# A reordered opening for a gated cross-attention and mixture-of-experts block: first loads on two queues, key spreading on GpSimd

## The reference

```python
def reference(x, ctx, g_xattn, g_ffn, ...):
    # cross-attention: 16 heads of 16 features, 77 context tokens per batch
    q = split_heads(layernorm(x) @ W_q.T + b_q)
    k = split_heads(ctx @ W_k.T + b_k)
    v = split_heads(ctx @ W_v.T + b_v)
    probs = softmax(einsum('bhsd,bhtd->bhst', q, k) / sqrt(16))
    x = x + tanh(g_xattn) * (combine(einsum('bhst,bhtd->bhsd', probs, v)) @ W_o.T + b_o)
    # feed-forward: a shared expert and two of seven routed ones per token
    h = layernorm(layernorm(x)) * ln_g + ln_b
    top_vals, top_idx = top_k(h @ Wr, 2)              # gates = softmax(top_vals)
    # each expert takes at most 732 (token, choice) slots
    routed = scatter_add(gate * (silu(xe @ W1) * (xe @ W3)) @ W2)
    shared = silu(h @ W1s) * (h @ W3s) @ W2s
    return x + tanh(g_ffn) * (routed + shared)
```

## Time and profile before

| what | us |
|---|---|
| median of 3 runs (878.12 to 883.29) | 878.38 |
| the profiled execution | 886.02 |
| its span, first to last instruction | 883.8 |
| PE busy | 839.1 (95%) |
| DVE busy | 590.3 (67%) |
| ACT busy | 387.7 (44%) |
| POOL busy | 320.2 (36%) |

### The profile page before, as it was taken

The page is one execution under the profiler, slowest core; times in us unless marked ns, Lnnn a source line. Parts: engine busy times, 40 slices in busy tenths (PEclk is TensorE's granted clock), DMA queues, the critical chain, the costliest instruction groups (busy, mean ns, idle before and its releaser), DMA issues.

```text
span 883.8 us, 14663 instructions
## 1 busy us (share of the span) xinstructions
PE 839.1 (95%) x5262; PEld 729.9 (83%) x5262; DVE 590.3 (67%) x1292; ACT 387.7 (44%) x717; POOL 320.2 (36%) x243
## 2 busy tenths in 40 slices
PE   8788999999999999999999999999999999999991
PEld 7465685886858868688688899999999999999990
DVE  4565768878778787888877576565656657565340
ACT  5425426345363263533725445353544445453330
POOL 4830303033012150031224603818375472814333
PEclk9788799999999999999999999999999999999996
DMA  6632041311412214112130722334434332431111
GB/s 227 163 72 64 11 120 36 98 35 39 119 37 66 65 38 119 36 39 62 33 120 11 215 84 80 65 106 95 114 83 86 101 79 69 101 65 20 17 19 19
DMA packets 93984, 66.93 MB, mean 76 GB/s; under 512 B 55110, under 2 KB 80892, under 8 KB 93928
## 3 DMA queue, kind: packets, MB, share of 16 engines
q1 hardware_dynamic: 40312, 55.40, 22.1%
q0 software_dynamic: 53088, 10.30, 8.5%
q10 hardware_dynamic: 528, 0.52, 0.2%
HBM read 37.38 MB, written 14.27 MB: 58 GB/s over the span
## 4 chain that ended last, share of the span: by engine, by line
PE 81%; issue 3%; ACT 3%; DVE 3%; POOL 1%; DMA 0%; DVEq 0%; ACTq 0%; POOLq 0%
PE bank L1608 21%; PE bank L1610 21%; PE bank L1609 21%; PE bank L1840 3%; PE bank L1841 2%; PE bank L1842 2%; PE bank L1732 2%; PE bank L1726 2%; DVE row_max L1278 2%; PE bank L1696 2%; ACT float_data L1100 1%; ACT probabilities L1100 1%; PE bank L1882 1%; PE bank L1794 1%; PE bank L1803 1%
## 5 line engine op out<-in xcount | busy, mean ns | idle before, releaser
L1608 PE MATMUL bank<-split_operands 128*128 128x366 f32 (+4 forms) x1148 | 383.6, 334 | 4.0 <-POOL split_operands L919 2.3
L1609 PE MATMUL bank<-split_operands 128*128 128x366 f32 (+4 forms) x1148 | 377.8, 329 | 0.0
L1610 PE MATMUL bank<-split_operands 128*128 128x366 f32 (+4 forms) x1148 | 377.6, 329 | 0.0
L1608 PEld LDWEIGHTS bank<-split_operands 128*128 128x128 f32 (+1 forms) x1148 | 215.6, 188 | 24.3 <-issue 9.0
L1610 PEld LDWEIGHTS bank<-split_operands 128*128 128x128 f32 (+1 forms) x1148 | 215.4, 188 | 12.3
L1609 PEld LDWEIGHTS bank<-split_operands 128*128 128x128 f32 (+1 forms) x1148 | 215.8, 188 | 9.6
L1018 POOL DMA_INDIRECT out<-float_data,scatter_now x42 | 125.7, 2994 | 185.6 <-DVE float_data L1571 108.7
L1591 DVE TENSOR_TENSOR hidden<-bank,float_data 128x366 f32<-128x366 f32 x112 | 60.4, 540 | 114.1 <-PE bank L1610 114.1
L1197 ACT ACTIVATE float_data<-bank 128x366 f32<-128x366 f32 x112 | 53.5, 477 | 113.7 <-PE bank L1610 113.7
L1194 ACT CAST split_operands<-hidden 128x366 fp32r<-128x366 f32 x112 | 55.7, 497 | 68.4 <-DVE hidden L1591 68.4
L993 POOL DMA_INDIRECT float_data<-z_scratch,gather_now x42 | 72.8, 1733 | 17.4 <-issue 16.2
(11 more groups left out here) (156 smaller groups left out, 1062.9 us busy)
## 6 DMA issues: line engine op xcount, KB each, us to landing
float_data<-in_L_ffn_W SPq DMA_DIRECT2D x21, 1024.0 KB, 8.7
split_operands<-split_operands SPq DMA_DIRECT2D x96, 128.0 KB, 2.3
float_data<-in_x SPq DMA_DIRECT2D x8, 512.0 KB, 4.3
z_scratch<-float_data SPq DMA_DIRECT2D x8, 512.0 KB, 3.1
out<-float_data SPq DMA_DIRECT2D x7, 512.0 KB, 2.9
split_operands<-split_operands SPq DMA_DIRECT2D x8, 192.0 KB, 3.8
float_data<-in_L_ffn_W1s SPq DMA_DIRECT2D x2, 512.0 KB, 9.8
float_data<-in_L_ffn_W3s SPq DMA_DIRECT2D x2, 512.0 KB, 8.0
```

Of the source, the lines that this page charges most:

```text
L1608: pe.matmul(o, lhs[0], rhs[0], start=first, stop=False)
L1609: pe.matmul(o, lhs[0], rhs[1], start=False, stop=False)
L1610: return pe.matmul(o, lhs[1], rhs[0], start=False, stop=last)
```

## The change

- The first loads go out on two queues: ACT issues the context, the keys' weights and the queries' weights; SP issues the tokens of block 0 first, then the rest.
- The keys are put into `kbd` by POOL, as a product with a mask of the rows of each head (`own_head`, `spread_keys`), in place of the zeroing and the eight DMAs on SP.
- The eight DMAs of the queries' hi parts are issued by ACT (`stack_hi`); SP keeps the four of lo parts.
- POOL's splits of the shared weights stand elsewhere: none beside the maxima, one piece after the scaling of block 1 and five after the values; the other pieces after the projection's operands and after `norm2`. ACT's hi parts move with them. `sh_stage` has other places, and the waits of the loads (`load_shared`) differ.
- `first_period` and `second_period` are in another order: `stats_x` of block 0 stands ahead of `context`, that of block 1 ahead of the queries; `transpose_x(n)` ahead of the first scores; `queries(n)` behind the scores; `maxima(n, 3)` in the second period; `up(2)` ahead of the scores of block 1; `keep_busy` appears at other places, with other counts.
- `queries`, `project` of block 0 and `up(0)` compute with the hi part of the moving operand first, so that they start before its lo part is there (`hi_first`, `project_first`, `first_up`). `maxima(b, 0)` waits for the queries' hi part alone. Banks are changed to suit.

```diff
 def first_period(do, b):
     n = b.next()
-    do("keep_busy", 2, 18, "ident_ready", 1)
+    do("keep_busy", 2, 14, "ident_ready", 1)
+    do("stats_x", b)
+    do("rest_const")
     do("context")
     do("weights", 1)
     do("project_keys")
-    do("keep_busy", 2, 4, "ident_ready", 1)
-    do("stats_x", b)
-    do("weights", 0)
     do("scale_x", b)
+    do("weights", 0)
     do("bias_keys")
+    do("spread_keys")
     do("transpose_x", b)
     do("weights", 2)
-    do("keep_busy", 2, 4, "ident_ready", 1)
+    do("stats_x", n)
     do("queries", b)
     do("keep_busy", 3, 4, "ident_ready", 1)
     do("queries_out", b)
+    do("residual", b)
     do("keys", b)
-    do("residual", b)
+    do("stack_hi", b)
     do("stack", b)
-    do("shared_weights")
-    for t in range(TT):
-        do("maxima", b, t)
-        if t == 1:
-            do("keep_busy", 6, 4, "xl_ready", KD)
-        if t == 2:
-            do("project_values")
+    do("shared_hi", 0, 2)
+    do("maxima", b, 0)
+    do("maxima", b, 1)
+    do("project_values", 0, 1)
+    do("maxima", b, 2)
+    do("project_values", 1, 2)
+    do("maxima", b, 3)
+    do("project_values", 2, B)
     do("maxima_T", b)
-    do("keep_busy", 4, 8, "m_done", TT)
     do("stack_maxima", b)
+    do("shared_hi", 2, 3)
+    do("scale_x", n)
+    do("shared_lo", 0, 1)
+    do("values_out")
+    do("shared_lo", 1, 6)
+    do("transpose_x", n)
     do("more_shared")
-    do("values_out")
-    norm(do, n)
+    do("keep_busy", 2, 8, "m_done", TT)
     do("first_scores", b)
-    do("transpose_x", n)
     do("route_const")
     do("scores", b, 0)
-    do("shared_hi", 3, 5)
-    do("shared_lo", 6, 10)
+    do("scores", b, 1)
     do("queries", n)
-    do("scores", b, 1)
+    do("attention_hi", b)
+    do("project", b)
     do("queries_out", n)
     do("stack", n)
+    do("shared_hi", 3, 6)
+    do("shared_lo", 6, 10)
+    do("project_out", b)
     do("maxima", n, 0)
+    do("keep_busy", 2, 15, "m_done", TT)
+    do("norm2", b)
     do("maxima", n, 1)
-    do("attention_hi", b)
...
 @block.sync
-        sp.dma_start(ctx_f.rearrange("p k b t -> p (k b t)"), a["ctx"]).then_inc(sig["ctx_loaded"], 16)
-        load_attention(1, 2, sig["wk_loaded"])
         sp.dma_start(xb[0], x_rows[0]).then_inc(x_loaded[0], 16)
         sp.dma_start(small[:, :], a["small"]).then_inc(sig["small_loaded"], 16)
-        load_attention(0, 1, sig["wq_loaded"])
...
 @block.scalar
+        act.dma_start(ctx_f.rearrange("p k b t -> p (k b t)"), a["ctx"]).then_inc(sig["ctx_loaded"], 16)
+        act.dma_start(watt_stage[:, 1:2], a["att"][:, 1:2]).then_inc(sig["wk_loaded"], 16)
+        act.dma_start(watt_stage[:, 0:1], a["att"][:, 0:1]).then_inc(sig["wq_loaded"], 16)
...
+        def spread_keys():
+            pool.wait_ge(sig["heads_ready"], 1)
+            for k in range(KD):
+                pool.wait_ge(sig["k_hi"], k + 1)
+                pool.tensor_tensor(kbd[:, k], k_s[:, 0, k, 0:SK].bitcast(F32).unsqueeze(1).broadcast_to([P, 8, SK]),
+                                   own_head[:, :].unsqueeze(2).broadcast_to([P, 8, SK]), ALU.mult)\
+                    .then_inc(sig["kbd_spread"], 1)
```

241 lines of the change are left out of this document (145 added, 96 removed).

## The result

The kernel after takes 873.82 us (median of 22 runs, 866.96 to 878.7); the kernel before, measured beside it, 878.61 (22 runs, 876.65 to 888.25). The ratio is 0.9925, with a 95% interval of 0.9904 to 0.9946. By the medians that is 4.8 us faster, by the ratio 6.6, where I had forecast 13.0 and 865.4 us. It is a gain, but one within the 1% that the prediction took as the least that can be told, an outcome to which it had given 0.31. The profiled executions tell another story: 886.02 before, 872.56 after, 13.5 apart.

A forecast was written before the change was run, and what follows sets the result against it. PE, busy 95% of the span, was taken as the bound, with losses in the opening reaching the end one for one. 3.7 + 11.5 + 1.8 - 1.5 - 1.5 - 1.0 = 13.0, so 878.38 - 13.0 = 865.4 us, range 856 to 876.

The forecast's parts named there:

- Stage A: Opening up to block 0's first scores: 0.8 + 1.2 + 1.7 = 3.7 us gained, scores at 29.5.
- The start charge: Before the keys: later loads, statistics first and slower keys cost 1.5 us, bounds 0 and 3.6; keys start near 10.5.
- Stage B: First scores to end of block 0's projection: 28.5 falls to 17.0, 11.5 us gained, 6.7 of it clock.
- the first rival: Block 0's scores: the clock falls at the first scores all the same, 6.1 us lost, 871.5; chance 0.24.
- Stage C: Projection's end to `up(0)`: eight of twelve products go ahead of the lo part, 1.8 us gained.
- The charges: Losses at the start, between projection and `up(0)`, and in the second period: 1.5, 1.5 and 1.0 us.
- The stretch behind the projection: Between projection and `up(0)`: one slow stretch of 3.1 us at half speed costs 1.5, bounds 0 and 3.
- The third: Second period: only `up(3)` and the transpose cover the way from last `pv` to POOL's lo part; 1.0 lost, bounds 0 and 1.5.
- The collisions: POOL splits beside DVE operations: at most four lie on stage B's chain; moving the splits was given no gain.
- second stretch gone: Around block 1's scores: the slow stretch of 82.4 to 99 goes too, giving 859.3; chance 0.13.
- Slow issues on ACT: Opening: ACT's DMA issues at double price make the first scores 6 us later, less the slack: 870.5; chance 0.08.
- the other side: Opening: PE's clock drops early and stays low until `up(1)`, 17.0 us more, 882.4; chance 0.05.

The follow-up runs named there:

- after_again: The changed kernel once more, with no edit: 875.92 us, ratio 0.9915 to the kernel before.
- hold_clock_before: The kernel before with 25 identities in place of 8 ahead of block 0's first scores: 879.42 us, ratio 0.9979.
- before_two_held: The kernel before with 17 more identities ahead of block 0's first scores and 10 behind the second period's logits' transpose: 879.14 us, ratio 0.9989.
- hold_clock_after: The changed kernel with 22 identities in place of 8 ahead of the first scores: 872.25 us, ratio 0.9884.
- stack_on_sp: The changed kernel with the eight stacking DMAs of the queries' hi parts issued by SP again: 878.77 us, ratio 0.9973.
- less_filler: The changed kernel with 17 identities in place of 8 ahead of the first scores and 10 behind the second period's logits' transpose: 868.38 us, ratio 0.986.
- all_held: The changed kernel with 19 identities for 14 at the start, 22 for 8 ahead of the scores, 10 behind the second period's logits' transpose: 869.61 us, ratio 0.9874.
- loads_one_queue: The changed kernel with all first loads issued on SP again, in the old order: 873.07 us, ratio 0.9919.
- queries_between: The changed kernel with block 1's queries back between the halves of block 0's scores: 879.46 us, ratio 0.9964.
- all_held_up_late: all_held with `up(0)` waiting for the lo part before its first product: 872.62 us, ratio 0.992.
- splits_beside_norm: The changed kernel with POOL's five splits waiting for the second `pv`, so that they run beside the divisions: 874.09 us, ratio 0.9918.

## Why the prediction was wrong

**The step that failed first: the baseline.** "The median of the runs shown is 7.6 lower; I take the change as the same number of us there." The offset is no constant. Of the 117 runs of before made beside the experiments, 60 have a mean clock of 0.971 to 0.978 and average 883.4 us, and 56 have 0.982 to 0.989 and average 877.4. Of 29 runs of the kernel after, 13 have 0.969 to 0.973 and average 877.2; 15 have 0.978 to 0.982 and average 871.8; one has 0.990 and took 866.96. The two groups are 6.0 us apart in the kernel before and 5.4 in the one after, which fits one long slow stretch more or less. In the profiles it is the second: after_again's has it (877.52 us), that of the kernel after has not (872.56). For before this rests on hold_clock_before and before_two_held, not on a profile of the kernel itself, and for single runs it is inferred, since in the new order the lack of the first stretch gives the same mean clock (hold_clock_after). Like against like the change gives 883.4 - 877.2 = 6.2 and 877.4 - 871.8 = 5.6: a steady 6 us, and the ratio says 6.6. The profiled pair compared the top of the slower group of before (886.02) with the faster group of after (872.56), and so showed 13.5. That this is close to the 13.0 of my sum is luck: its parts were others, as follows.

**The account by stages, like against like.** All four other profiles of before and after_again have the second stretch. Between them the first scores start 4.4 us earlier in the mean, the way from there to the projection's end is 1.1 shorter, the way on to `up(0)` 1.8 shorter, and the way from `up(0)` to block 1's projection 2.0 longer (33.9 us, before 31.7 to 32.1). That makes 5.3, and the spans differ by 5.5. From the start of block 1's projection to the end every profile in this document has 779.7 to 780.9 us, so all of the change lies ahead of it. I had 3.7 + 11.5 + 1.8 - 4.0. The term that was mis-sized is B, by some 10 us.

**Stage A, forecast 3.7, measured 3.1 to 5.** Against the other four profiles of before, whose first scores start at 33.6 to 35.1, the 30.11 is 3.5 to 5.0 earlier. The parts were off in both directions. ACT's issues cost 0.66 each (taken 0.69), and the spreading on POOL 1.4 (taken 1.5), covered as foreseen. The start charge was not paid. My sum had the copy issued at 27.2 and landed 2.3 us later; it was issued at 25.22 and landed 4.8 us later. What I left out is that the twelve stacking transfers and the copy share what the DMA engines carry. The Trainium skill (DMA: Bandwidth & Descriptors, "Issuing engines are not separate DMA queues") says that DMAs interleave on the same 16 engines whichever engine starts them. I had weighed that rule at the first loads, where it mattered little, and not here, where stack_on_sp and the landing rows of the stacking DMAs (2.3 us from one issuing engine, 4.9 from two) agree with it.

**Stage B, forecast 11.5, measured 6.2 in the profiled pair** (28.5 before, 22.3 from 30.11 to the projection's end at 52.4)**.** The step that failed is "here `transpose_x(n)` and keep_busy's 8 identities fill up to about 28.5, and one idle us is left". The filling ended at 27.8 and the idle was 2.28, so the clock fell: the first rival, to which I had given 0.24 and 871.5 us. That filling this gap and some more keeps the clock, less_filler, hold_clock_after and all_held show. That the idle time alone brings the fall is not shown: loads_one_queue and queries_between fell without it. The arithmetic under it holds: less_filler goes from first scores to projection in 13.6 us, and I had 13.7 (29.5 to 43.2). And the 6.7 us of clock that I credited were seldom there to be won. In the other four profiles of before the way from first scores to the projection's start takes 19.0 to 19.5 us, not 23.8; in the two profiles of the kernel after, 19.3 and 20.2. Against them the change gains nothing on that way; only the projection itself is shorter, 3.0 us in place of 4.2 to 5.5, which before ran at the low clock.

**Stage C, forecast 1.8, measured 1.8** (52.4 to 60.91 is 8.5, before 10.35). all_held_up_late puts it at 3.0, of which the longer wait is 1.9. This term was right, and it is the same in every pair of profiles: 10.35 us from the projection's end to `up(0)` in all five of before, 8.5 in both of after.

**The charges.** The start (1.5, bounds 0 and 3.6) was 0: the tokens landed at 5.57, the keys started at 9.34, 0.8 later than before, and the queries' products at 12.89, 1.9 sooner than before. The stretch behind the projection (1.5, bounds 0 and 3) was 0 in both profiles. The third (1.0, bounds 0 and 1.5) measured 0.62 + 0.91 = 1.5. The second period as a whole is 2.0 us longer than before, and 2.9 where its clock stays up (29.5 us, hold_clock_before 26.6): `maxima(n, 3)` now stands there, `up(0)` waits 0.78 for its lo part, and PE waits 1.75 for the first exponentials of block 1, in hold_clock_before 0.91. I had taken off 4.0 in charges and 2.0 were paid, so they do not explain the miss; alone they would have made the gain larger than forecast.

**The collisions.** I gave nothing for them, and that held. The reductions of block 0's maxima, first before, with POOL's splits beside them, then after, without:

```profile
L1278 DVE TENSOR_REDUCE row_max<-bank 128x6 f32<-128x462 f32 x8 | 4.7, 631 | 2.2 <-PE bank L1696 2.2
```

```profile
L1300 DVE TENSOR_REDUCE row_max<-bank 128x6 f32<-128x462 f32 x8 | 4.7, 632 | 0.2 <-PE bank L1731 0.2
```

631 and 632 ns: POOL did not slow them. The division with two SBUF operands is what it slows (0.42 to 1.31 us in splits_beside_norm). The Trainium skill (GPSIMD Engine Reference, the table of specifications) names contention for VectorE instructions with two SBUF inputs, and both rows agree.

**The rivals.** The first was the median's case. The second (second stretch gone, 859.3) is half right: by the two groups that stretch is absent in about half of the runs of either kernel, so it was a part of the noise, not of the change. My 865.4, which still had that stretch in it, was too low even for a clock that never falls: less_filler, with no slow stretch, takes 868.4. Without low clock and unpaid charges my sum from the profiled execution comes to 886.02 - 13.0 - 6.1 - 3.0 = 863.9, and less_filler's profiled execution took 866.98. Of the 3.1 us between, 0.8 are there at `up(0)` (55.88, by the sum 55.05), and about 1.9 come in the second period, 2.9 longer where I had taken 1.0. Slow issues on ACT and the other side were wrong.

What stays open: why about the same idle time ends in a slow stretch of 3.4 us in one profile and of 13.6 in another, and why the clock fell in two profiles with almost none; which stretch the runs of before near 877 us lack, since none was profiled; why the copy lands 2 us sooner when it is issued a few tenths later; and what the order alone is worth at a clock that never falls, since no profile of the old order is free of slow stretches.

## What to carry to other kernels

Before a gain is worked out from a slow-clock stretch, look at whether the other runs have it: the mean granted clock of each run sorts them, and a profile from one group must not be set against a median from the other. Where a clock is expected to hold, fill the idle time in front of the thin work up to the moment when its last operand really lands, and look at several executions, since the same filling held in one variant and not in two others; nine identities more there, and ten behind block 1's first scores, took the kernel after from 873.82 to 868.38 us (ratios to before 0.9925 and 0.986), while filler in the old order brought little (879.14) or lost 6 us (884.4, where PE had to wait in front of it). The same ten identities cost 2.3 us ahead of the first scores of a block, where the exponentials wait for them, and 0.4 behind them, where PE waits anyway. Issuing small transfers from two engines brings them forward, but count their landing at the shared rate and not at the time that each took alone.

## What was not expected of the hardware

- One and the same program has slow stretches in some executions and not in others: in before, 60 of 117 runs carry about 6 us more than the rest, at a mean clock lower by about 0.01.
- A stretch of low clock begun near the first scores lasted 13.6, 3.5, 3.4, 6.8 and 3.4 us in five profiles of the same kernel, and 17.0 in both of the kernel after.
- The landing of a 64 KB copy inside SBUF was 2.3 us behind transfers issued by one engine and 2.3 to 4.8 us where two engines issued, the long ones in the four profiles that issued it soonest.
